# A Flamingo layer on one core: another order for the start of the first batch

## The reference

```python
def layer(x, ctx, mask):
    q, k, v = (heads(n @ W + b) for n, W, b in ((_layernorm(x), Wq, bq), (ctx, Wk, bk), (ctx, Wv, bv)))
    s = q @ k.T / 8
    s = where(mask, -1e30, s); s = where(causal(256, 1601), -1e30, s)
    x = x + tanh(g_attn) * ((softmax(s) @ v) @ Wo + bo)
    n = _layernorm(x); e = argmax(n @ Wr + br)
    # every expert i runs on n * (e == i): relu(. @ W1[i] + b1[i]) @ W2[i] + b2[i], and all are added
    return x + tanh(g_ffn) * sum_of_experts(n, e)
```

## Time and profile before

| | us |
|---|---|
| median of 3 runs (lowest, highest) | 389.42 (386.71, 389.92) |
| the profiled execution | 390.34 |
| its span, first to last instruction | 388.4 |
| PE busy in the span | 359.2 (92%) |
| DVE, ACT, POOL busy | 281.7, 247.1, 190.5 |

### The profile page before, as it was taken

One profiled execution on the slowest core, in us unless ns is written; L12 is line 12 of the kernel. 1 busy time (PEld: TensorE's weight loads), 2 busy tenths in 40 slices (PEclk: granted clock), 3 DMA queues, 4 the chain that ended last, 5 costly groups with the idle time before them and its releaser, 6 DMA issues.

```text
span 388.4 us, 11201 instructions
## 1 busy us (share of the span) xinstructions
PE 359.2 (92%) x2829; PEld 289.0 (74%) x2829; DVE 281.7 (73%) x1301; ACT 247.1 (64%) x907; POOL 190.5 (49%) x367
## 2 busy tenths in 40 slices
PE   3969998999999999999999999999999998868793
PEld 2847777677877787788788777877777777858793
DVE  6189993889598959886885889597946667654672
ACT  1766876587587667775875787487653547434562
POOL 7037463357446644664366356446644430516454
PEclk9999999999999999999999999999999989969999
DMA  6898202000200200020003001200019203122320
GB/s 212 193 364 222 84 4 86 3 0 11 106 0 0 84 27 0 0 87 25 0 0 112 0 0 28 97 0 0 0 56 402 117 27 97 49 62 83 94 73 12
DMA packets 20938, 27.34 MB, mean 70 GB/s; under 512 B 3545, under 2 KB 16677, under 8 KB 20912
## 3 DMA queue, kind: packets, MB, share of 16 engines
q1 hardware_dynamic: 19408, 23.88, 19.5%
q0 software_dynamic: 1504, 3.16, 2.4%
HBM read 18.48 MB, written 9.01 MB: 71 GB/s over the span
## 4 chain that ended last, share of the span: by engine, by line
PE 81%; DVE 5%; issue 3%; DMA 3%; ACT 3%; SPq 1%; another core or an unknown queue 1%; POOL 1%; POOLq 0%; DVEq 0%; ACTq 0%
PE ps_kv L1172 16%; PE ps_o L1172 14%; PE ps_s L1172 13%; PE ps_t L1245 11%; PE ps_w L1172 10%; PE ps_q L1172 8%; PE ps_t L1172 6%; DVE masked L752 2%; PE ps_s L1367 1%; DMA w_in<-in_L_xattn_Wv 1%; DMA out<-tile_out,tile_in 1%; ACT prob L553 1%; DMA tile_in<-sorted_rows 1%; PE ps_w L1277 1%
## 5 line engine op out<-in xcount | busy, mean ns | idle before, releaser
L426 POOL TENSOR_SCALAR prob<-prob,row_inv 128x128 f32<-128x128 f32 (+1 forms) x256 | 104.0, 424 | 144.7 <-DVE row_inv L765 144.7
L553 ACT ACTIVATE prob<-masked,neg_max 128x128 f32<-128x128 f32 (+1 forms) x256 | 113.4, 444 | 68.9 <-DVE neg_max L752 68.9
L752 DVE CUSTOM_DVE_ANT_0 masked<-ps_s,mask_now 128x128 f32<-128x128 f32 (+1 forms) x256 | 78.8, 353 | 24.6 <-PE ps_s L1172 20.7
L771 DVE COPY prob_T<-ps_t 128x384 f32<-128x384 f32 x128 | 67.5, 548 | 1.8 <-issue 1.6
L1172 PE MATMUL ps_s<-k_T,q_T 64*128 64x128 f32 (+1 forms) x512 | 59.3, 350 | 1.9 <-DVE neg_max L752 1.8
L1245 PEld LDWEIGHTS ps_t<-ident,prob 128*128 128x128 f32 x384 | 41.6, 142 | 22.6 <-issue 16.5
L1245 PE MATMUL ps_t<-ident,prob 128*128 128x128 f32 x384 | 57.0, 284 | 1.5 <-DVE prob_T L771 1.3
L1172 PE MATMUL ps_o<-prob_T,v_nat 128*64 128x256 f32 (+1 forms) x512 | 56.2, 340 | 0.0
L553 ACT ACTIVATION_READ_ACCUMULATOR prob<-masked,neg_max 128x1 f32 x256 | 47.9, 187 | 0.0
L1172 PEld LDWEIGHTS ps_o<-prob_T,v_nat 128*64 128x64 f32 x512 | 31.3, 137 | 17.6 <-issue 2.9
L497 POOL DMA_INDIRECT out<-tile_out,tile_in x23 | 23.2, 1009 | 41.2 <-DVE tile_out L1119 29.6
(11 more groups left out here) (195 smaller groups left out, 570.0 us busy)
## 6 DMA issues: line engine op xcount, KB each, us to landing
ctx_buf<-in_ctx SPq DMA_DIRECT2D x8, 768.0 KB
sorted_rows<-pad_rows SPq DMA_DIRECT2D x8, 642.5 KB, 4.5
tile_in<-sorted_rows SPq DMA_DIRECT2D x24, 128.5 KB, 2.2
packs<-in_L_ffn_W SPq DMA_DIRECT2D x1, 2048.0 KB
packs<-in_L_ffn_W SPq DMA_DIRECT2D x8, 256.0 KB
nat<-in_ctx SPq DMA_DIRECT2D x8, 128.0 KB, 3.9
nat<-in_x SPq DMA_DIRECT2D x1, 896.0 KB, 9.3
w_in<-in_L_xattn_Wk SPq DMA_DIRECT2D x1, 512.0 KB, 4.1
```

The source lines that it names most:

```text
L426: g.tensor_scalar(prob[:, slot, lo:hi], prob[:, slot, lo:hi], row_inv[:, slot, t:t + 1], 1.0, ALU.mult, ALU.mult).then_inc(prob_ready, 1)
L553: s.activation(prob[:, slot, lo:hi], masked[:, slot % 2, lo:hi], ACT.Exp, bias=neg_max[:, slot, t:t + 1], scale=-1.0, accum_out=row_sum[:, ...
L752: v.tensor_tensor_reduce(out=masked[:, slot % 2, lo:hi], in0=ps_s[slot % 2][:, lo:hi], in1=mask_now[:, lo:hi], scale=-SCALE, scalar=FLOOR, ...
L771: v.tensor_copy(prob_T[:, slot % TSLOTS, :], ps_t[slot % 2][:, 0:W3]).then_inc(probT_kept, 1)
```

## The change

1. Loads: Wk, Wq and Wv come in halves of 512 columns (`HALF`; pairs 0 to 3 and 4 to 7), the first halves first; the mask of batch 0 alone (`ld_mask0`) and x of batch 1 (`ld_x1`) come early, the other rows of the mask later. The four bias rows are issued from ScalarE's queue.
2. GpSimd: the fills of `sel` and `pad_rows` wait until x_norm of batch 0 is written; `others_p` and the fill of `ctx_buf` go ahead of them.
3. TensorE: the order is key 0, transposes of x, key 1, query 0, values 0, scores 0, values 1, and then the rest of the projections with scores 1 and 2 among them. Keys of pairs 0 and 1 go to ps_t0 and ps_t1, their values both to ps_o (`first_k`, `first_v`), with semaphores of their own.
4. ScalarE: exponentials lie among the evictions of keys and values; it evicts only queries 6 and 7 (`q_last`). VectorE evicts queries 0 to 5 (`q_first`).
5. VectorE: mask_now of batch 0 right behind the norm; the norm of batch 1 is spread over its waits and is done before `keep_probT` of pair 0; sums of pairs 0 and 1 come earlier.
6. Counts: q_act and q_dve start with batch 1, kv_done with pair 2; the waits on them are moved accordingly.

```diff
 # SP
-            sp.dma_start(wk_s[:, :], wk).then_inc(ld_wk, 16)
...
+            sp.dma_start(wk_s[:, 0:HALF], wk[:, 0:HALF]).then_inc(ld_wk[0], 16)
+            sp.dma_start(wq_s[:, 0:HALF], wq[:, 0:HALF]).then_inc(ld_wq[0], 16)
+            sp.dma_start(mask_all[:, 0, :], mask[0:1, 0:S].partition_broadcast(P)).then_inc(ld_mask0, 16)
+            sp.dma_start(wv_s[:, 0:HALF], wv[:, 0:HALF]).then_inc(ld_wv[0], 16)
+            sp.dma_start(x_d[:, 1], x_v[:, 1]).then_inc(ld_x1, 16)
+            sp.dma_start(wk_s[:, HALF:], wk[:, HALF:]).then_inc(ld_wk[1], 16)
+            sp.dma_start(wv_s[:, HALF:], wv[:, HALF:]).then_inc(ld_wv[1], 16)
+            sp.dma_start(wq_s[:, HALF:], wq[:, HALF:]).then_inc(ld_wq[1], 16)
+            sp.dma_start(mask_all[:, 1:B, :], mask[1:B, 0:S].partition_broadcast(P)).then_inc(ld_mask, 16)
 # GpSimd
+            g.memset(ctx_buf[:, FULL, :], 0.0).then_inc(tails_zero, 1)
+            pool.wait_ge(xnorm_ready, QT)
+            n.up(g.memset(sel[:, :, :], 0.0))
+            n.up(g.memset(pad_rows[:, :, :], 0.0))
+            n.wait()
             g.affine_select(out=sel[:, :, :], in_=sel[:, :, :], compare_op=ALU.not_equal,
                             fill=1.0, base=0, pattern=[[-1, E], [0, P]], channel_multiplier=1
                             ).then_inc(const_ready, 1)
...
+            g.memset(pad_rows[:, :, 2 * D:ROW].bitcast(i32), NOBODY).then_inc(const_ready, 1)
 # ScalarE
+            for i, b_ in enumerate((bq, bk, bv)):
+                act.dma_start(bias_rows[i * PAIRS:(i + 1) * PAIRS, :],
+                              b_.rearrange("(n p) -> n p", p=P)).then_inc(ld_bias, 16)
...
+            first_k(0)
+            act.wait_ge(inT_done, 1)
+            s.activation(xT, ps_s[1][:, 0:S], ACT.Copy).then_inc(inT_ready, 1)
+            first_k(1)
+            first_v(0)
+            first_v(1)
+            exponentials(0)
+            for j in range(2, 4):
+                keep_kv(j, j, kv_banks[(j - 2) % 3])
+            exponentials(1)
+            for j in range(4, PAIRS):
+                keep_kv(j, j, kv_banks[(j - 2) % 3])
+            exponentials(2)
+            for j in range(PAIRS - 2, PAIRS):
+                last_q(j)
 # VectorE
             normalise_x(0)
+            dve.wait_ge(ld_mask0, 16)
+            dve.wait_ge(const_ready, 2)
+            mask_of(0)
+            dve.wait_ge(biasT_ready, 1)
...
+            first_q(0)
+            dve.wait_ge(ld_x1, 16)
+            norm_stats(1)
+            norm_sums(1)
+            next_norm(0, 1, 2, 3)
+            first_maximum(0)
+            first_q(1)
+            next_norm(4, 5)
+            first_q(2)
+            first_sums(0)
+            first_maximum(1)
+            first_q(3)
+            next_norm(6, 7)
+            first_q(4)
+            next_norm(8)
+            first_maximum(2)
+            first_sums(1)
+            next_norm(9, 10, 11)
+            first_q(5)
+            for h in range(2):
+                keep_probT(0, h, h)
+            dve.wait_ge(ld_x[1], 16)
             dve.wait_ge(ld_mask, 16 * 2)
             dve.wait_ge(const_ready, CONSTS)
 # TensorE
             def first_kv(j):
 
+                if j < 4:
+                    pe.wait_ge(k_kept, j - 1)
+                elif j == 4:
+                    pe.wait_ge(v_kept, 2)
+                    pe.wait_ge(ld_wk[1], 16)
+                    pe.wait_ge(ld_wv[1], 16)
+                else:
+                    pe.wait_ge(k_kept, j - 2)
+                    pe.wait_ge(v_kept, j - 2)
+                keys_and_values(j, kv_banks[(j - 2) % 3])
...
+            pe.wait_ge(ld_wk[0], 16)
+            first_k(0)
+            pe.wait_ge(xnorm_ready, QT)
+            for t in range(QT):
+                last = t_.transpose(ps_s[1][:, t * P:(t + 1) * P], x_norm[:, t, :], ident[:, :])
+            last.then_inc(inT_done, 1)
+            first_k(1)
+            pe.wait_ge(inT_ready, 1)
+            first_q(0)
+            pe.wait_ge(ld_wv[0], 16)
+            first_v(0)
+            scores(0, 0, 0)
+            first_v(1)
+            first_kv(2)
+            first_q(1)
+            first_kv(3)
+            first_q(2)
+            scores(1, 1, 0)
+            first_kv(4)
+            first_q(3)
+            first_kv(5)
+            first_q(4)
+            scores(2, 2, 0)
+            first_kv(6)
+            first_kv(7)
+            for j in range(5, PAIRS):
+                first_q(j)
             pe.wait_ge(const_ready, CONSTS)
+            pe.wait_ge(v_kept, PAIRS - 1)
             for h in range(2):
                 transpose_probs(0, h, h)
+            pe.wait_ge(v_kept, PAIRS)
             batch(0, first=True)
```

More of the change, by code:

```diff
@@ L268, in flamingo_layer @@
         q_act, q_dve = sem("q_act"), sem("q_dve")
+        k01_done, v01_done = sem("k01_done"), sem("v01_done")
+        q_first, q_last = sem("q_first"), sem("q_last")
         scores_done, max_ready, exp_done = sem("scores_done"), sem("max_ready"), sem("exp_done")
@@ L1064, in _, with first_q, first_maximum @@
             normalise_x(0)
+            dve.wait_ge(ld_mask0, 16)
+            dve.wait_ge(const_ready, 2)
+            mask_of(0)
+            dve.wait_ge(biasT_ready, 1)
+            def first_q(j):
+                dve.wait_ge(q_done, j + 1)
+                v.tensor_scalar(q_T[:, j, :], q_banks[j % 3][:, 0:S], bias_T[:, j:j + 1], None, ALU.add
+                                ).then_inc(q_first, 1)
+            def first_maximum(p):
+                for h in range(2):
+                    maximum(p, h, 2 * p + h)
@@ new lines, in first_sums, with next_norm @@
+            def first_sums(p):
+                fix_sums(p, 2 * p)
+                invert_sums(p, 2 * p)
+            def next_norm(*steps):
+                for step in steps:
+                    norm_scales(QT, 2 * QT, step)
+            first_q(0)
[8 more added lines that the diff above has]
+            first_sums(0)
@@ L1065, in _ @@
+            first_maximum(1)
[7 more added lines that the diff above has]
+            first_q(5)
+            for h in range(2):
+                keep_probT(0, h, h)
+            dve.wait_ge(ld_x[1], 16)
             dve.wait_ge(ld_mask, 16 * 2)
             dve.wait_ge(const_ready, CONSTS)
-            mask_of(0)
-            dve.wait_ge(biasT_ready, 1)
@@ L1069, in _ @@
[L1069 to L1086, removed]
@@ L1177, in input_transposes @@
                 pe.wait_ge(ctxnow_ready, b)
-                pe.wait_ge(q_act, 4 * b)
-                pe.wait_ge(q_dve, 4 * b)
+                all_q_kept(b - 1)
                 for t in range(QT):
@@ L1184, in input_transposes, with all_q_kept @@
                 last.then_inc(inT_done, 1)
+            def all_q_kept(b):
+                if isinstance(b, int) and b == 0:
+                    pe.wait_ge(q_first, PAIRS - 2)
+                    pe.wait_ge(q_last, 2)
+                else:
+                    pe.wait_ge(q_act, 4 * b)
+                    pe.wait_ge(q_dve, 4 * b)
             def q_kept(b, j):
                 if Q_ON_ACT(j):
-                    pe.wait_ge(q_act, 4 * b + j // 2 + 1)
+                    pe.wait_ge(q_act, 4 * (b - 1) + j // 2 + 1)
                 else:
-                    pe.wait_ge(q_dve, 4 * b + j // 2 + 1)
+                    pe.wait_ge(q_dve, 4 * (b - 1) + j // 2 + 1)
             def project_q(b, j):
@@ L1230, in scores @@
                 pe.wait_ge(k_kept, p + 1)
-                q_kept(b, j)
+                if not isinstance(b, int) or b > 0:
+                    q_kept(b, j)
+                elif j < PAIRS - 2:
+                    pe.wait_ge(q_first, j + 1)
+                else:
+                    pe.wait_ge(q_last, j - PAIRS + 3)
                 wait(pe, max_ready, 4 * p)
@@ L1327, in last_projection @@
                 if c == 0:
-                    pe.wait_ge(q_act, 4 * B)
-                    pe.wait_ge(q_dve, 4 * B)
+                    all_q_kept(b)
                 pe.wait_ge(oT_kept, 8 * b + c + 1)
```

90 lines of the change are left out of this document (37 added, 53 removed).

## The result

| | before | after |
|---|---|---|
| median of 6 runs, us | 388.95 | 382.05 |
| lowest, highest | 384.47, 390.82 | 379.86, 383.27 |
| profiled execution's span | 388.4 | 381.4 |

The ratio is 0.984 (0.980 to 0.988), some 6.3 us of 389 (4.8 to 7.7): faster by over 1%. The forecast was 384.2 with 382.0 to 388.0. The measured 382.05 lies inside by 0.05 us, and outside the forecast's own range of 383.0 to 386.0. The spans of the two profiles are 7.0 us apart.

What follows compares the result with a forecast made beforehand. TensorE was taken as the bound, with only the first 33.6 us affected. Batch 1's first projection comes 6.2 us earlier, less 1.0 for gaps: gain 5.2, so 389.42 - 5.2 = 384.2 us, range 382.0 to 388.0.

Steps and rivals of the forecast that it cites:

- The norm, 6.8: VectorE's first norm, freed of GpSimd's fills, saves 2.44 us: x_norm written at about 6.8 instead of 9.25.
- The fills beside VectorE cost nothing: Moved fills run from 6.8 to 10.1 beside VectorE without charge; 0.9 us worse if every fill holds every operation.
- Loads cost 0: Halved weights and early loads land before needed in the start; bound +1 us, later loads within 0.5 either way.
- The new order: TensorE's reordered start: scores 3 at 22.8 for 26.76, first projection of batch 1 at 27.4 for 33.61, 6.2 us earlier.
- the mark: Start of batch 1's first query projection on TensorE, where its steady order begins; 33.61 us before the change.
- VectorE no longer late: Transposed probabilities of pair 0 kept at 23.1, maxima 3 done by 25.0, scores 4 at about 25.6 for 31.52.
- The gain reaches the end whole, the rest is unchanged: Behind batch 1's first projection TensorE has hardly a gap, so the start's gain should reach the end whole.
- rival (c): Later stretches give the start's gain back through lower clock, two more such stretches making 388.8 us; chance 0.06.
- The number: Whole kernel: gain 5.2 us, 384.2 us from a median of 389.42; own range 383.0 to 386.0, wider 382.0 to 388.0.
- (a): In the start the softmax chain on ScalarE binds, not TensorE; gain only 3.0 us, 386.4; chance 0.20.
- (b): Context load for GpSimd's sum, wanted at 25.6, lands late; at 28 the gain is 2.4 less, 386.6; chance 0.08.
- (d): TensorE's broken start delays full speed, 0.5 us per us behind 12.1; 393.9 if the switch is at 31.5; chance 0.04.

Runs made afterwards that it cites:

- e1: Changed kernel with GpSimd's fills of sel and pad_rows back in their old place; 0.993 (0.987 to 0.998) of the time before.
- e7: The changed kernel measured again with no edit; 0.989 (0.986 to 0.993) of the time before, in 12 runs.
- e8: e5 with the four bias rows issued from SP again; profiled span 381.0 us, against 378.7 for e5.
- e5: Changed kernel with 17 needless identity transposes added in TensorE's pauses before x_norm; 0.987 (0.982 to 0.993) of the time before.
- e13: e5 measured again with no edit; 0.982 (0.977 to 0.987) of the time before.
- e11: e5 with eight more needless transposes on TensorE ahead of query 5; profiled span 382.7 us, against 378.7 for e5.
- e10: e5 with three needless copies on ScalarE behind the exponentials of pair 2; profiled span 381.9 us, against 378.7 for e5.

## Why the prediction was right, and where it was off

- *The norm, 6.8.* Measured 6.85; the saving of 2.44 is 2.40. e1 gives it back to 0.01. The reading of the three slow steps against the fills was right.
- *The fills beside VectorE cost nothing.* Right: mask_now beside the fill of sel took 0.62 for its two operations, the same as in e1 with no fill beside it, and first_q(0) and the statistics of the next norm beside the selection on sel took their usual 0.48 and 0.47. So the harsher reading of the earlier trace rows (every fill holds every operation; 0.9 us) is refuted for these operations. The Trainium skill, SBUF — State Buffer, section Who interferes with whom, says that an operation with two SBUF inputs meets only a GpSimd instruction that reads SBUF; mask_now has two and the fill only writes, so the trace agrees here.
- *Loads cost 0.* Right for the changed kernel: none of its first weights was waited for. There is little to spare: in e7 mask_now waited 0.46 us for its row of the mask, at no cost, and e8's wait for half of Wv is 0.39 us.
- *The new order.* Scores 0 10.09 for 9.75, scores 3 23.58 for 22.8, scores 4 26.63 for 25.6, the projection 28.59 for 27.4, before the 1.0 that I took off for gaps. With it the gain at the mark was forecast as 5.2; it is 5.0, and 5.95 in e7. The gaps are there, as waits of 0.2 to 0.4 us of TensorE's weight loads for ScalarE and GpSimd; the slow pace until 12.1 was assumed and came in the first profile by luck of that execution.
- *VectorE no longer late.* Scores 3 to scores 4: 2.8 forecast, 3.05 measured, 4.76 before. The prediction had scores 4 wait for maxima. The rows of before have no wait there; TensorE's wait, 1.32 us for VectorE, lies ahead of the transposes of pair 1. The engine was right, the place was not.
- *The gain reaches the end whole, the rest is unchanged.* This step was off. From the mark to the end it took 354.8 us before and 352.8 after. Up to the first tile 0.7 was lost (289.3 for 288.6 us from the mark); over the fourteen profiles this distance lies between 288.6 and 290.7. The last stage took 66.2 us in the profile of before and 63.5 after. The fourteen profiles have it between 61.6 and 66.4, and two profiles of one kernel lie at both ends (e5, e13). So of the 6.9 us between the medians some 5 are of the change and the rest is chance, as the second measurement (4.1 us) bears out. I had looked at this stage only as rival (c), as a place to lose.
- *The number.* The gain at the mark, 5.2, was right, and by the mechanism that was forecast. That 382.05 lies in the range is luck. The lower end, 382.0, was to stand for no gaps and a switch 2 us earlier; neither came in the first profile. It was also added up wrong: 5.2 + 1.0 + 1.0 is 7.2 and not 7.4, and 389.42 - 7.2 is 382.2, which would have left 382.05 outside. Of the 2.15 us between it and the forecast 0.5 is the median of before (388.95 instead of 389.42), and the rest, some 1.7, is less than the 4.8 us by which the last stage varies. The second measurement, 383.60, lies 0.6 below the forecast and in its own range, but the interval of its ratio (0.986 to 0.993) no longer shows that the gain is over 1%.
- *The rivals.* (a) is refuted up to the mark, on the version with the added transposes: e11 costs its full work, e10 only what exceeds 0.56 us. (b) did not occur; how much earlier the context's load lands than 27.3 was not measured. (c) did not occur as a loss, but for the 0.7 us up to the first tile. (d) did not occur, but its price, half a us per us of delay, is what e7 shows.

The last stage of e5 and of e13, columns as in the earlier trace rows:

```profile
317.10:378.70 61.60, 48.03 (x409) 45.62 (x407) 37.10 (x132) 32.33 (x120) 25.35 (x25) 0.99 0.22 65
```

```profile
315.70:382.10 66.40, 52.11 (x409) 49.66 (x407) 37.79 (x132) 32.23 (x120) 25.24 (x25) 0.91 0.23 66
```

The same instructions, at a granted clock of 0.99 and 0.91, keep PE busy for 48.0 and 52.1 us. That goes some way to explain 61.6 against 66.4. It does not explain the 2.7 us between the first two profiles: there the granted clock was 0.94 for 66.2 us before and 0.91 for 63.5 after, and PE busy 50.9 and 50.2. e11 has 0.95 and 66.0. What makes the difference was left open.

## What to carry to other kernels

An edit to a start is priced by the chain of the order in which it will stand: moving GpSimd's fills was worth 0 us in the old order and 2.4 at the first scores in the new one. When work is rearranged so that the bound engine never waits, follow the second engine's list too, and test by adding work to each: the slip tells the slack. Read the slip at later marks too: e10's was 0.36 us at the mark and 0.94 two turns on. Compare starts by marks in the traces before believing medians that another stage moves by several us, and note in each trace when the full pace comes: with it at the same time 0.02 us repeat (e5, e13), with it 2 us apart one kernel's marks lie 0.93 apart.

## What the runs showed of the hardware

The granted clock in the profile reads 1.00 from the start, while matmuls run at half the pace, in the seven profiles without added transposes until 9.3 to 14.5 us: 0.86 us for a projection of 256 columns instead of 0.43. By durations that is the lower level, 1.2 GHz. The pace changed at 10 in one execution of the changed kernel and at 12 in another, with PE's rows equal to 0.01 us between 6.9 and 10.1 and differing by up to 0.25 before. It seems to move with the work, in part: it came 2.5 us later in the one profile of e1, where the work from the transposes of x on began 2.4 later, and by 5.6 in four of seven executions with transposes from 1.57 on.

In the last stage the granted clock does fall in the records (0.67 over 340 to 350 before, 0.84 after), and how much differs from one execution to the next: over the whole stage it is 0.90 to 0.99 in the fourteen profiles.

Three small operations of VectorE (128x2 and 128x4, 0.16 us alone) took 0.98 us beside GpSimd's selection, 1.32 beside a plain fill and 1.67 beside a sum, and each ended within 0.04 us of GpSimd's. Three larger ones passed beside the fill of sel or the selection at their usual time (0.62 for two, 0.48, 0.47).
